# A two-layer cross-attention kernel on one core: the first layer's output products moved by one slot, and the first batch's products and roundings put in another order

## What is computed

```
q = x @ Wq;  k, v = text @ Wk, text @ Wv;  k_ip, v_ip = ip @ Wk_ip, ip @ Wv_ip
text_out = softmax(q_h k_h^T / 4) v_h
fused    = q_h k_ip_h^T / 4 + 0.5 * sem
ip_out   = softmax(fused) * mask @ v_ip_h
x        = (text_out + ip_out) @ Wout + bias + x
```

## Time and profile before

| what | value |
|---|---|
| median of 3 runs | 1632.13 us |
| lowest and highest run | 1630.63 and 1632.45 us |
| the profiled execution's own time | 1630.7 us |
| its span | 1628.7 us |
| TensorE matmul busy | 1560.4 us (96%) |
| VectorE busy | 1393.6 us (86%) |
| ScalarE busy | 1015.7 us (62%) |
| GpSimd busy | 717.3 us (44%) |
| mean granted TensorE clock | 0.982 |

### The profile page before, as it was taken

The page is one execution under the profiler, slowest core; times in us unless marked ns, Lnnn a source line. Parts: engine busy times, 40 slices in busy tenths (PEclk is TensorE's granted clock), DMA queues, the critical chain, the costliest instruction groups (busy, mean ns, idle before and its releaser), DMA issues. The chain is left out here.

```text
span 1628.7 us, 42423 instructions
## 1 busy us (share of the span) xinstructions
PE 1560.4 (96%) x13960; PEld 1385.5 (85%) x13960; DVE 1393.6 (86%) x4083; ACT 1015.7 (62%) x2444; POOL 717.3 (44%) x629
## 2 busy tenths in 40 slices
PE   6999999999999999998999999999999999999986
PEld 5888888888888888777798888988898889898876
DVE  4687787877888888876899999999999999999995
ACT  3455556566565655655667767667676776676652
POOL 3234432223322322433556655655555565565442
PEclk9999999999999999998999999999999999999998
DMA  8334444444444444443324323332333233332311
GB/s 228 99 107 118 123 128 131 119 125 129 122 127 125 117 127 125 135 123 109 88 82 123 102 76 111 106 101 72 104 104 105 75 103 96 104 99 71 94 38 36
DMA packets 204098, 175.29 MB, mean 108 GB/s; under 512 B 45312, under 2 KB 203402, under 8 KB 203882
## 3 DMA queue, kind: packets, MB, share of 16 engines
q1 hardware_dynamic: 203882, 172.59, 36.8%
HBM read 112.12 MB, written 60.38 MB: 106 GB/s over the span
## 5 line engine op out<-in xcount | busy, mean ns | idle before, releaser
L1061 POOL TENSOR_TENSOR ZS<-ZP 128x256 f32<-128x256 f32 x267 | 275.4, 1032 | 279.7 <-DVE ZP L968 279.7
L616 ACT ACTIVATE P<-TA 128x512 f32<-128x512 f32 x320 | 202.3, 632 | 278.4 <-DVE TA L956 275.2
L336 PE MATMUL NAT<-KS,QS 65*128 65x256 f32 x1280 | 299.2, 316 | 7.6 <-ACT SC L570 5.5
L978 DVE SCALAR_TENSOR_TENSOR PM<-P,PH 128x512 f32<-128x512 f32 x320 | 275.2, 860 | 0.0
L350 PE MATMUL TR<-QS,KS 69*128 69x256 f32 (+2 forms) x1280 | 258.7, 284 | 4.3 <-DVE TA L956 2.1
L144 PE MATMUL GP<-PH,GH 128*128 128x256 f32 x936 | 241.7, 288 | 17.6 <-DVE ZP L968 17.3
L336 PEld LDWEIGHTS NAT<-KS,QS 65*128 65x128 f32 x1280 | 201.1, 192 | 63.3 <-issue 48.4
L863 DVE TENSOR_REDUCE MX<-NAT 128x2 f32<-128x504 f32 x320 | 215.8, 675 | 34.6 <-PE NAT L336 31.1
L284 POOL TENSOR_TENSOR PARTS<-QKF,PARTS 112x512 fp32r<-112x512 f32 (+1 forms) x93 | 121.5, 1307 | 278.4 <-ACT PARTS L646 233.3
L144 PE MATMUL GP<-PH,GL 128*128 128x256 f32 x936 | 236.3, 281 | 0.0
L619 ACT ACTIVATE P<-TR 128x512 f32<-128x512 f32 x320 | 193.0, 603 | 59.0 <-PE TR L350 58.2
(11 more groups left out here) (269 smaller groups left out, 3817.4 us busy)
## 6 DMA issues: line engine op xcount, KB each, us to landing
QS<-qk_parts SPq DMA_DIRECT2D x480, 64.0 KB
KS<-qk_parts SPq DMA_DIRECT2D x480, 64.0 KB
qk_parts<-PARTS SPq DMA_DIRECT2D x128, 224.0 KB, 2.9
CT<-in_ctx_t SPq DMA_DIRECT2D x32, 512.0 KB, 3.9
qk_parts<-PARTS SPq DMA_DIRECT2D x64, 192.0 KB, 2.4
XT<-in_x_t SPq DMA_DIRECT2D x48, 112.0 KB, 2.6
XT<-x_t SPq DMA_DIRECT2D x48, 112.0 KB, 2.4
XB<-in_x SPq DMA_DIRECT2D x16, 320.0 KB, 4.0
```

The source lines that it names most:

```text
L336: ins = e.matmul(NAT[s % 2][:, i * T:(i + 1) * T], QS[0:KQ, h, i * 128:(i + 1) * 128], KS[0:KQ, h, :], start=True, stop=True)
L616: e.activation(P[:, s % NP, :], TA[:, s % 2, :], ACT.Exp, scale=SCALE).then_inc(q["exp"], 1)
L978: e.scalar_tensor_tensor(PM[:, s % 2, :], P[:, (S1 + s) % NP, :], 2.0, PH[:, s % NS, :].bitcast(F32), ALU.mult, ALU.subtract).then_inc(q[" ...
L1061: e.tensor_tensor(ZS[s % NZ][:, :], ZP[:, s % 2, 0:S], ZP[:, s % 2, S:2 * S], ALU.add).then_inc(q["zs"], 1)
```

## The change

It edits the slot tables and makes the table entries per batch count for q and cts too.

1. `om` goes from offsets (64, 67) to (63, 66) and `y` from (65, 68) to (64, 67). The three last batches have entries of their own, which stay, so this concerns batches 0 to 12.
2. For batch 0 the three q products stand together in the slot of the first (offset -9, slot -29), ahead of all its k products; the rounding of its context moves from slot -21 to slot -19.
3. ONCE goes from slot -6 to slot -17; the store of its values stays in slot -6 under a name of its own (VALL_OUT).
4. The roundings of the value weights go from slots -27 and -23 to -17 and -16. The value products of batch 0 now wait for their own weight each.
5. The rounding of the output weights goes from slot -8 to slot 6.

```
-AT0 = dict(... om=(64, 67), y=(65, 68), yt=(72, 73), out=69, out_t=74)
+AT0 = dict(... om=(63, 66), y=(64, 67), yt=(72, 73), out=69, out_t=74)
...
-LATE0 = {B - 3: dict(om=(62, 66), y=(63, 67), out=68, yt=(74, 75), out_t=76),
+OWN0 = {0: dict(q=(-9, -9, -9), cts=1), B - 3: dict(om=(62, 66), y=(63, 67), out=68, yt=(74, 75), out_t=76),
...
-NORM, ONCE = -9, -6
+NORM, ONCE, VALL_OUT = -9, -17, -6
...
-FILL0, WV0, WO0 = 4 - H, (-7 - H, -3 - H), -8
+FILL0, WV0, WO0 = 4 - H, (3 - H, 4 - H), 6
...
-            for m in range(3):
-                for b in both(t, AT0["q"][m], AT1["q"][m]):
+            for m in range(3):
+                for b in fore(at0(t, "q", m), of1(t, AT1["q"][m])):
...
+                    if b == 0 and n < 2:
+                        e.wait_ge(q["w_lo"], 2 + n)
                     if n == 0:
-                        if b == 0:
-                            e.wait_ge(q["w_lo"], 3)
                         e.wait_ge(q["ct_lo"], b + 1)
...
-            b = of0(t, AT0["cts"])
+            b = at0(t, "cts")
...
-            for b in both(t, AT0["cts"], AT1["cts"]):
+            for b in fore(at0(t, "cts"), of1(t, AT1["cts"])):
...
-            if t == ONCE:
+            if t == VALL_OUT:
                 e.wait_ge(q["once_s"], 3)
                 e.dma_start(vall, VALL).then_inc(q["vall_out"], 16)
```

More of the change, by code:

```diff
@@ L42 @@
 AT0 = dict(q=(-9, -5, -1), k=(-8, -4, 0), spill=(-7, -3, 1), x_in=-22, xts=-14, c_in=-15, cts=-1, tl=2, norm=3, g0=3, tpt=4,
-           sem=6, v=(10, 14, 18), xb_in=53, num=44, hst=49, htl=50, om=(64, 67), y=(65, 68), yt=(72, 73), out=69, out_t=74)
+           sem=6, v=(10, 14, 18), xb_in=53, num=44, hst=49, htl=50, om=(63, 66), y=(64, 67), yt=(72, 73), out=69, out_t=74)
 AT1 = dict(q=(0, 4, 9), k=(1, 5, 10), spill=(2, 6, 11), x_in=-22, xts=-9, c_in=-15, ctn=-4, cts=-2, v=(6, 8), gr=(12, 13), gl=(13, 14),
@@ L78, in at0 @@
     for b in range(B):
-        off = LATE0.get(b, AT0).get(name, AT0[name])
+        off = OWN0.get(b, AT0).get(name, AT0[name])
         for n in at:
```

## The result

| kernel | median | runs | profiled execution | its span |
|---|---|---|---|---|
| before | 1630.63 us | 5 (1626.64 to 1632.45) | 1630.7 us | 1628.7 us |
| changed | 1640.61 us | 5 (1636.97 to 1642.02) | 1640.61 us | 1638.8 us |

The ratio is 1.0066 with a 95% interval of 1.005 to 1.0081: about 10.8 us slower (10.0 by the two medians), where 6.1 us faster was forecast.

The account below looks back on a forecast made before the run. TensorE was taken to set the pace in the first layer. Thirteen waits regained (-3.6), the front (-5.6) and the output weights' rounding (+3.15) summed to -6.05 us: median 1626.0 us, range 1619.0 to 1632.0.

Parts of the forecast that it names:

- That fits by 0.2 us, and costs nothing: Slot 9: GpSimd's HS chain, 1.3 us later, ends at 330.0, before the first transposes want it at 330.21; no cost.
- the other half, in slots 3 and 4: Output product ahead of slot 4's NAT makes its maxima 1.3 us later; VectorE's 1.18 us idle absorbs nearly all.
- two slots and the product of 1.32 us lie between, so I count nothing: Slot 4's transpose takes the bank of slot 2's semantic logits; enough time lies between, so no cost.
- The wait of L306: Slot 9: HS transposes wait for the addition L843, 0.69 us in each of thirteen batches; the earlier addition removes it.
- The addition ahead of slot 7's maxima: Slot 7: delays the exponential about 0.40 us, so 0.28 of 0.69 us remains per batch, 3.6 us gained over thirteen.
- The front: Start up to the first TR: -4.7 + 0.5 - 1.4 = -5.6 us, between -3.4 and -7.5.
- The first NAT: Expected at 33.1 us, 0.5 later than 32.57, within 32.0 to 33.8.
- The chain up to it: From the last k product's end to the first NAT, with ONCE's products put there: 11.7 us.
- The clock stayed at the upper level: Value products, 34 to 36 us: with ONCE in the pauses TensorE's clock is at its upper level, 1.4 us gained.
- The rounding in slot 6: Output weights' rounding delays the next slot's maxima, so NAT waits and TensorE idles: +3.15 us, between 1.0 and 4.5.
- The slower one: Rival, chance 0.10: GpSimd's HS comes too late for slot 9's first transposes; +5 us, 1637 us.
- the empty-front rival: Rival, chance 0.16: the start gives nothing net, through a later semantic chain or a clock falling elsewhere; 1631.6 us.

Follow-up runs that it names:

- TPT first: Changed kernel with ScalarE's copy of TPT (batches 1 to 15) ahead of its slot's exponential: ratio 0.9955 to before, 1621.58 us.
- half 1 alone: Kernel before with only the second offsets of om (67 to 66) and y (68 to 67) moved: ratio 0.9971, 4.7 us faster.
- front alone: Changed kernel with om and y back at offsets (64, 67) and (65, 68): ratio 0.9975 to before, about 4.1 us faster.
- TPT first, rounding in slot 11: Changed kernel with TPT's copy ahead of the exponential and the output weights' rounding in slot 11: ratio 0.9937 to before, 1618.40 us.

## Why the prediction was wrong

**The step that failed** is "That fits by 0.2 us, and costs nothing", on the other half, in slots 3 and 4. Its times were right: with the shift of 0.65 us taken off, HS ends at 330.01, as reckoned, and TensorE does not wait for it. What it left out is who else is touched by GpSimd's chain moving 1.3 us later: the cost of VectorE's L884 was put at nothing without a reason. I asked only who reads GpSimd's result. In both kernels L884 starts inside GpSimd's addition and lasts until it ends. The change moved that end 1.32 us later and L884's start only 0.36, so it takes 1.39 instead of 0.44 us, at a point where the exponential, and behind it PV, had 0.74 us to spare. The sign to read was in the trace of before: the same instruction 0.44 us long in slot 6, 1.32 us in the first batch, and 0.17 in most other places. I did not look at it.

The Trainium skill has the rule ("SBUF — State Buffer", section "SBUF: two separate sides"): of a VectorE instruction with two SBUF inputs and a GpSimd instruction that reads SBUF, whichever starts first keeps the shared port pair for its whole instruction, and the other is blocked. The prediction cited it for the output weights' rounding, where it did not matter (1.16 us there, without a competitor), and not for the step that moves GpSimd's work. The runs agree with it, the order of starting included (0.17 us when first, 1.39 when second). That TA, with one input in PSUM, took its usual 0.68 us beside GpSimd's addition (both start at 323.14 in the rows with TPT first) agrees too.

**Also missed:** "two slots and the product of 1.32 us lie between, so I count nothing" dealt with a bank; the copy of TPT behind a later exponential on ScalarE was not in the sum. It makes about 0.35 us by itself, and with the order of L884 and GpSimd's addition 1.51.

**What was right.** The wait of L306 goes (it did). The addition ahead of slot 7's maxima delays the exponential by 0.40 and leaves 0.28 of 0.69 us: half 1 alone gave 0.29, period 42.84 us. Thirteen of these are 3.6 us; measured with half 1 alone, 4.7, with an interval from 2.8 to 6.7.

**The front.** The first TR came 7.8 us earlier instead of 5.6. From the first NAT to it are 17.18 us now and 23.65 before: 6.5 less, for 4.7 and 1.4 reckoned. The first NAT was mis-sized: 31.28 instead of 33.1, 1.3 us earlier than before rather than 0.5 later. The chain up to it was right (11.87 us for 11.7); the last k product ends at 19.41, where 20.3 to 22.1 was taken. The clock stayed at the upper level, as taken. The rounding in slot 6 made a pause of 3.32 us, for 3.15 reckoned, by the chain that was named; VectorE's part is 1.16 us, for 1.1 to 1.46. The sum for the front and that rounding, -2.45, was in fact about -4.1 (front alone), and the loss of the period, 13 x 1.02 = 13.3 us, outweighed it: together +9.2, for a measured 10.8 with an interval from 8.2 to 13.2.

**The rivals.** The slower one was near and yet the wrong way round: it had GpSimd held off by VectorE and TensorE waiting for HS. The engine that was held was VectorE, and no wait for HS appears. Its 0.10 was too little for a step whose own margin I had put at 0.2 us. The slow stretch of the empty-front rival came (0.57 from 64 to 72 us), but before has one as deep without that pause (0.58 from 72 to 80 us), and the front alone still gained.

## What to carry to other kernels

With the wait for TPT that decided the order, this made 1.51 us per period (44.15 against 42.64), about 19 us over thirteen periods; the instruction alone made 1.18 of it, about 15 us. And useful work put into TensorE's pauses can pay twice: ONCE in slot -17 took 4.7 us out of a full stretch, and in the front-only kernel the clock from 32 to 40 us was 1.00 instead of 0.70, together 7.9 us to the first TR. The clock isn't sure to follow: in one kernel with ONCE in slot -17 (TPT first, rounding in slot 11) it was 0.82 there.
